# Sorting the tokens on chip with a permuting transposition instead of through rows in DRAM

## The reference, cut to what matters

```python
h = _layernorm(x, axis=-1) * (1 + ca) + sa
x = x + ga * _L0_attn_ref(h, ...)
h = _layernorm(x, axis=-1) * (1 + cb) + sb
x = x + gb * _L0_ffn_ref(h, ...)
...
logits = x_flat @ w_router.T
probs = jax.nn.softmax(logits, axis=-1)
top_idx = jnp.argmax(probs, axis=-1)
top_weight = jnp.take_along_axis(probs, top_idx[:, None], axis=1)[:, 0]
h = jnp.einsum('nd,ehd->enh', x_flat, w_fc)
a = jnp.square(jnp.where(h >= 0, h, 0.5 * h))
expert_out = jnp.einsum('enh,edh->end', a, w_proj)
```

## Time and profile before

| | |
|---|---|
| median of 3 runs | 616.06 us (613.67 to 618.61) |
| profiled execution | span 626.6 us; no other time of it is shown |
| instructions | 11028 |
| PE busy | 545.7 us (87%) |
| DVE busy | 394.7 us (63%) |
| ACT busy | 282.3 us (45%) |
| POOL busy | 209.2 us (33%) |
| moved by DMA | 61.40 MB |

### The profile page before, as it was taken

How to read it: one execution, slowest core, us unless ns; L and a number is a source line. 1 busy time by engine, 2 the same in 40 slices (tenths; PEclk the granted TensorE clock), 3 DMA queues, 4 the chain that set the end, 5 groups by cost and what they waited for, 6 DMA issues and landing times.

```text
span 626.6 us, 11028 instructions
## 1 busy us (share of the span) xinstructions
PE 545.7 (87%) x3052; PEld 441.0 (70%) x3052; DVE 394.7 (63%) x801; ACT 282.3 (45%) x679; POOL 209.2 (33%) x185
## 2 busy tenths in 40 slices
PE   5989959494528899999999999999999999998860
PEld 0435444453327899999999999999999999987750
DVE  3697889898893565454555545555545455567862
ACT  2668583532114455454445445455445445432320
POOL 1030276684886121122122122122112212157541
PEclk9999969789658999999999999999999999999996
DMA  8911543030267520201201202202101010077641
GB/s 314 390 69 52 217 152 120 0 137 1 84 235 236 222 69 2 70 16 51 69 0 67 67 0 67 67 0 67 64 3 67 6 61 0 0 242 245 182 143 67
DMA packets 17042, 61.40 MB, mean 98 GB/s; under 512 B 3051, under 2 KB 3051, under 8 KB 13688
## 3 DMA queue, kind: packets, MB, share of 16 engines
q1 hardware_dynamic: 11256, 42.63, 19.3%
q0 software_dynamic: 5760, 18.43, 8.2%
HBM read 47.30 MB, written 14.27 MB: 98 GB/s over the span
## 4 chain that ended last, share of the span: by engine, by line
PE 71%; DVE 11%; issue 8%; ACT 3%; DMA 2%; another core or an unknown queue 2%; POOL 1%; DVEq 0%; SPq 0%; ACTq 0%; POOLq 0%
PE bank L912 32%; PE bank L940 28%; PE bank L756 3%; DVE xc L1076 3%; PE bank L821 2%; DVE junk L1151 1%; PE bank L774 1%; PE bank L789 1%; PE bank L826 1%; DVE u L1089 1%; DMA sorted_tokens<-gap,gapI 1%; DVE st L1019 1%; DMA wm<-wmod 1%; DVE res L1126 1%
## 5 line engine op out<-in xcount | busy, mean ns | idle before, releaser
L490 POOL TENSOR_TENSOR Wlo<-raw,Whi (+1 forms) x64 | 82.3, 1290 | 276.4 <-ACT Whi L651 276.3
L912 PE MATMUL bank<-XShi,Whi 128*128 (+1 forms) x576 | 165.7, 288 | 5.7 <-DVE twice_h L1341 4.9
L912 PE MATMUL bank<-XShi,Wlo 128*128 (+1 forms) x576 | 164.1, 285 | 0.0
L912 PE MATMUL bank<-XSlo,Whi 128*128 (+1 forms) x576 | 164.1, 285 | 0.0
L1360 DVE TENSOR_TENSOR acc<-acc,bank 128x512 f32 (+1 forms) x126 | 85.9, 687 | 71.7 <-PE bank L940 66.6
L1341 DVE TENSOR_TENSOR twice_h<-relu_h,bank 128x256 f32<-128x256 f32 x144 | 60.2, 420 | 99.4 <-ACT relu_h L713 96.8
L912 PEld LDWEIGHTS bank<-XShi,Whi 128*128 128x128 f32 x576 | 111.6, 194 | 12.1 <-issue 9.8
L940 PE MATMUL bank<-Whi,ahi 128*128 128x512 f32 x272 | 107.9, 397 | 6.6 <-DVE alo L1349 6.5
L912 PEld LDWEIGHTS bank<-XSlo,Whi 128*128 128x128 f32 x576 | 111.6, 194 | 2.1
L912 PEld LDWEIGHTS bank<-XShi,Wlo 128*128 128x128 f32 x576 | 111.5, 194 | 0.0
L940 PE MATMUL bank<-Wlo,ahi 128*128 128x512 f32 x272 | 107.3, 394 | 0.0
(11 more groups left out here) (146 smaller groups left out, 605.9 us busy)
## 6 DMA issues: line engine op xcount, KB each, us to landing
raw<-wffn SPq DMA_DIRECT2D x16, 1024.0 KB, 5.2
wm<-wmod SPq DMA_DIRECT2D x6, 1024.0 KB, 12.4
res_row<-sorted_residuals SPq DMA_DIRECT2D x18, 260.0 KB
sorted_rows<-sorted_tokens SPq DMA_DIRECT2D x9, 512.0 KB, 10.8
x_in<-x SPq DMA_DIRECT2D x4, 1024.0 KB, 10.1
bc<-mod_rows SPq DMA_DIRECT2D x4, 772.0 KB, 7.0
ga_bc<-ga_rows SPq DMA_DIRECT2D x4, 256.0 KB, 3.5
wx_sb<-wx SPq DMA_DIRECT2D x1, 514.0 KB, 10.7
```

The costliest lines, as they stand in the source:

```text
L490: pool.tensor_tensor(Wlo[:, hb % 2, c, :], raw[:, c, :], Whi[:, hb % 2, c, :].bitcast(F32), ALU.subtract).then_inc(s_wlo, 1)
L912: mm = pe.matmul(hP[m][:, 0:TILE], W[wp][:, par, 2 * e + k // 2, o:o + P], XS[xp][:, k, bass.ds(t * TILE, TILE)], start=(n == 0), stop=(n ...
```

## The change

The sorted rows never go to DRAM. A token's place within its block of 128, from the front for one expert and from the back for the other, makes a 0/1 matrix `perm` (four DVE instructions per batch). PE's transposition of z2 takes it in the identity's place, so its result is channels by tokens with the tokens of a block in order: one expert's first, the other's last. ACT evicts this modulated (scale and bias per channel from `cols`) into a window of 128 columns of `XSfull` (channels by sorted tokens, four channel groups innermost) that starts at the front's running count, read from memory into a register; then the whole window is copied to the place that the count from the back gives. The next block overwrites what did not belong. In the last batch DVE makes the copies. POOL clears XSfull first. XShi and XSlo are made from XSfull, with no reload and no transpositions among the expert tiles.

Along with it: the margin comes from `res` times the router row before normalisation, corrected by two numbers per batch, so it no longer needs z2; the modulated router row (`wd_dram`) and the sums (`sc_dram`) are broadcast for all batches at once, and `margin_products(0)` waits for all five landings. POOL has no h2 work. The statistics of the first normalisation are all on DVE (`stats1`), in the places shown. The output of blocks uses two PSUM banks (`pO`) where four were used. Tap 2 of the next batch stands behind the margins and not before them. Ranks and positions of a batch stand together ahead of the next scan. `prefix(b)` stands behind all four transpositions of batch b+2 on PE. The residual rows are still scattered through DRAM.

```diff
...
+            def permuted_block(b, j):
+                n = TJ * b + j
+                if j < 2:
+                    pe.wait_ge(s_hT, KT * min(b + 3, NB))
+                wait(pe, s_e0, KT * (n - 1))
+                pe.wait_ge(s_pm, n + 1)
+                pe.wait_ge(s_z2, n + 1)
+                for k in range(KT):
+                    mm = pe.transpose(pT[j % 2][:, P * k:P * k + P], z2[:, j, P * k:P * k + P], perm[:, j, :])
+                mm.then_inc(s_pz, 1)
...
+            def place(b):
+
+
+                act.wait_ge(s_off, b + 1)
+                first = [act.value_load(offI[0:1, b % 2, j:j + 1], min_val=0, max_val=P * (TJ * b + j)) for j in range(TJ)]
+                if b == 0:
+                    act.wait_ge(s_fill, 1)
+                    act.wait_ge(s_cols, 3)
+                for j in range(TJ):
+                    n = TJ * b + j
+                    act.wait_ge(s_pz, n + 1)
+                    wait(act, s_e1, n)
+                    for k in range(KT):
+                        act.activation(XSfull[:, bass.ds(first[j], P), k], pT[j % 2][:, P * k:P * k + P], ACT.Identity,
+                                       bias=cols[:, 4, k, b:b + 1], scale=cols[:, 3, k, b:b + 1]).then_inc(s_e0, 1)
+                    if b < NB - 1:
+                        act.wait_ge(s_e0, KT * (n + 1))
+                        act.activation(XSfull[:, bass.ds(first[j] + (FROM_BACK - P * n), P), :],
+                                       XSfull[:, bass.ds(first[j], P), :], ACT.Copy).then_inc(s_e1, 1)
...
+            pool.wait_ge(s_wg, NB)
+            pool.wait_ge(s_mr, 7)
+            pool.wait_ge(s_mc, 3)
+            pool.wait_ge(s_md, 64)
+            pool.memset(XSfull[:, :, :], 0.0).then_inc(s_fill, 1)
...
+            def margin_products(b):
+                if b == 0:
+                    dve.wait_ge(s_bc, 16 * (NB + 1))
+                for j in range(TJ):
+                    dve.wait_ge(s_x2, TJ * b + j + 1)
+                    wait(dve, s_q, TJ * b + j)
+                    dve.tensor_tensor_reduce(junk[:, :], res[:, b % 2, j, 0:DM], bc[:, b, :], 1.0, 0.0, ALU.mult, ALU.add,
+                                             q[:, j:j + 1]).then_inc(s_q, 1)
...
+            def permutations(b):
+                wait(dve, s_pz, TJ * b)
+                for j in range(TJ):
+                    dve.tensor_scalar(perm[:, j, :], colidx[:, :], place_col[:, j:j + 1], None, ALU.is_equal).then_inc(s_pm, 1)
...
+            b = NB - 1
+            dve.wait_ge(s_off, NB)
+            first = [dve.value_load(offI[0:1, b % 2, j:j + 1], min_val=0, max_val=P * (TJ * b + j)) for j in range(TJ)]
+            dve.wait_ge(s_e1, TJ * b)
+            for j in range(TJ):
+                n = TJ * b + j
+                dve.wait_ge(s_e0, KT * (n + 1))
+                dve.wait_ge(s_e1, n)
+                dve.tensor_copy(XSfull[:, bass.ds(first[j] + (FROM_BACK - P * n), P), :],
+                                XSfull[:, bass.ds(first[j], P), :]).then_inc(s_e1, 1)
...
```

More of the change, by code:

```diff
@@ new lines, in build @@
+        woutg += [take(f"woutg{b}", [P, DM]) for b in range(2, NB)]
+        wout_sb = take("wout_sb", [P, DM])
+        wdb = take("wdb", [P, KT, P])
+        perm = take("perm", [P, TJ, P])
+        wm = [at(f"wm{n}", [P, KT, 512], F32, o) for n, o in enumerate((o_raw, o_raw + ZB, o_whi, o_whi + ZB, o_wlo, o_wlo + ZB))]
+        cur[0], limit[0] = o_acc, o_a
+        ga_bc = take("ga_bc", [P, NB, DM])
+        modrow = take("modrow", [NB, 6, DM])
+        wdrow = take("wdrow", [NB, DM])
+        scrow = take("scrow", [NB, SC])
@@ L246, in build @@
         s_gbc = sem("ga_broadcast_landed")
[L247 removed]
+        s_bc = sem("router_rows_landed")
         s_md = sem("mod_stored")
@@ L766, in mod_columns, with transposes1 @@
                 mm.then_inc(s_mc, 1)
-            def transposes1(b, ks=range(KT)):
-                for k in ks:
+            def transposes1(b):
+                for k in range(KT):
+                    if k < 2 and b >= 2:
+                        wait(pe, s_e0, KT * TJ * (b - 2))
                     wait(pe, s_hT, KT * b + k - 1)
@@ new lines, in prefix @@
+                pe.matmul(pO[0][:, TJ:2 * TJ], ones[:, :], m1[:, :], start=True, stop=True).then_inc(s_pf, 1)
+            def permuted_block(b, j):
[5 more added lines that the diff above has]
+                pe.wait_ge(s_z2, n + 1)
+                for k in range(KT):
+                    mm = pe.transpose(pT[j % 2][:, P * k:P * k + P], z2[:, j, P * k:P * k + P], perm[:, j, :])
+                mm.then_inc(s_pz, 1)
@@ L1280, in _ @@
                 if nxt:
-                    for k in range(KT):
-                        if k == 2:
-                            softplus_residue(b + 1)
-                        conv(b + 1, 2, (k,), taps)
-                        if newton_steps and k < 3:
-                            newton_steps[k + 1]()
+                    softplus_residue(b + 1)
+                if b == 0:
+                    own.link(mod_row(3, modrow[0:NB, 3, :], 1.0))
+                    dve.tensor_tensor_reduce(wdrow[:, :], modrow[0:NB, 3, :], wdiff[:, :], 1.0, 0.0, ALU.mult, ALU.add,
+                                             scrow[:, 1:2]).then_inc(s_mr, 1)
@@ L1307, in _ @@
-                margins(b)
-                if b == NB - 1:
-                    row_candidates(b)
-                    counts(b)
-                    ranks(b)
-                    positions(b)
+                    columns(3, 5, 3).then_inc(s_cols, 1)
+                if b == 1:
+                    newton1(3)
+                margin_products(b)
+                margins(b)
+                candidates(b)
+                if b == 0:
+                    mod_row(5, modrow[0:NB, 5, :], 0.0).then_inc(s_mr, 1)
+                    dve.wait_ge(s_mr, 6)
+                    clamp_row(5)
@@ L1314, in _ @@
+                if nxt:
+                    conv(b + 1, 2, range(KT), taps)
+                ranks(b)
+                permutations(b)
+                if b == NB - 1:
                     own.link(dve.tensor_scalar(n0f[:, :], run[:, :], -1.0, float(TOK), ALU.mult, ALU.add))
```

611 lines of the change are left out of this document (236 added, 375 removed).

## The result

The changed kernel takes 637.26 us (median of 4 runs, 635.92 to 637.76), the kernel before 617.19 on the same chip (4 runs, 613.67 to 618.61). The ratio is 1.034, 95% interval 1.030 to 1.038: 20.1 us slower. The forecast said 626.0, slower by 10.0, range 609 to 641. The direction and the range held; half of the loss was missing.

What follows compares the result with a forecast made beforehand. DVE was taken to bound the mixer, TensorE the experts. Start -0.4, three batch steps +13.4, +4.2 and -4.1, and tail -3.1 sum to +10.0 us on 616.06, so 626, range 609 to 641.

Steps and rivals of the forecast that it cites:

- Batch 0 to 1: Mixer step from batch 0's decayed state ready to batch 1's: 57.1 us where it was 43.7, +13.4.
- (a): Batch 0 to 1: with two output banks instead of four, DVE waits 4.2 us for delta product, Abs and Exp.
- (c): Batch 0 to 1: all five broadcasts of the packed rows must land, at 80.1 us against 72.77 before.
- (e): Batch 0 to 1: TensorE's prefix counts stand behind all transposes of batch 2, so ranks begin at 94.4 us.
- (g): Batch 0 to 1: state product behind the prefix, partly at TensorE's slow clock; together 5.6 us instead of 3.6.
- The tail: From the last state ready to the experts' effective start: 35.8 us where it was 38.9, -3.1.
- effective start: When expert block 0 would have begun if gapless up to the next block's first fc: 201.8 us before, forecast 211.8.
- rival C: Placing of sorted tokens on ACT is the bound, at 0.73 us an eviction: +25, 641 us; chance 0.13.
- The carried difference: Profiled span of before, 626.6 us, is 10.5 above the runs' median; carried over, giving 616.06 + 10 = 626.
- A: Mixer: DVE stays the bound and the new waits hide, under 4 us a batch: -10, 606 us; chance 0.15.
- B: No change: same chain with fast clock, overlapping register loads and quick broadcasts: +2, 618 us; chance 0.22.
- D: GpSimd's clearing of XSfull holds DVE's small copy of the ranks: +12 in all, 628 us; chance 0.10.

Runs made afterwards that it cites:

- Experiments 5: Changed kernel with tap 2 before the margin products, TensorE's prefix counts before the transposes, XSfull cleared after the first four permutations; 639.88 us, ratio to before 1.012 to 1.033.
- 9: Changed kernel with the edits of Experiments 5, 7, Experiment 2 and experiment 6 together; 617.00 us, ratio to the kernel before 0.980 to 0.996.
- Experiment 2: Changed kernel with GpSimd's four subtractions for weight chunks 4 to 7 delayed until the last block is copied; 642.14 us, ratio to before 1.013 to 1.028.
- Experiment 1: Changed kernel with the high and low passes reading XSfull contiguously, which permutes the tokens; 642.27 us, ratio to before 1.017 to 1.034.
- experiment 6: Changed kernel with block 0's high and low passes of tile t+2 behind tile t's squares and low part; 643.29 us, ratio to before 1.009 to 1.034.
- 10: Kernel 9 with GpSimd's four subtractions of chunks 4 to 7 also behind DVE's first four low passes; 610.29 us, ratio to before 0.991 to 0.997.
- 4: Changed kernel with the delta product before permuted blocks and outputs on TensorE, Abs and Exp before placing on ACT; 650.70 us, ratio to before 1.026 to 1.046.
- 7: As 4, with all four outputs of a batch also ahead of the third and fourth permuted block on TensorE; 641.61 us, ratio to before 1.016 to 1.043.

## Why the prediction was half right

*What bounds the kernel, the start, the three steps.* Right in place and size. Start -0.5 (forecast -0.4). Batch 0 to 1: 56.1 where it was 43.7, +12.4 (+13.4). Batch 1 to 2: +3.7 (+4.2). Batch 2 to 3: -4.2 (-4.1). The named waits of terms (a), (c) and (e) stand in the first step where they were put, in DVE's timeline of after:

```profile
63.58 0.43 DVE L968 TENSOR_SCALAR w<-eabs 128x512 f32<-128x512 f32 x1 [4.03 <-ACT eabs L529]
...
76.90 0.19 DVE L1081 COPY cols<-bank 128x32 f32<-128x32 f32 x1 [2.95 <-PE bank L689]
...
80.32 0.69 DVE L1020 CUSTOM_DVE_ANT_0 eabs<-res,bc 128x512 f32<-128x512 f32 x1 [3.23 <-DMA scal<-router_sums]
...
94.09 0.16 DVE L1043 TENSOR_TENSOR place_col<-cand,bank 128x4 f32<-128x4 f32 x1 [3.52 <-PE bank L748]
```

Product start 80.3 (80.1), ranks 94.1 (94.4). Experiments 5 and 9 confirm (c) and (e) by taking them away. Term (g) was too high in batch 0: the state product took 4.47, not 5.6, and the second Bu did not wait. The close agreement of the last step is partly luck: DVE had Exp's result 1.4 sooner after state ready than forecast and was 0.7 quicker from there to the end of the first Bu, but the state product of batch 3 took 6.47 us and held the second Bu for 1.94, which the sum did not have.

*The eviction* was 1.63 for four, 0.41 each; I had taken 0.40 against bounds of 0.32 and 0.73. The register loads on DVE began 0.73 apart (four from 193.0 to 195.2) where I had 0.8.

```profile
100.73 1.63 ACT L579 ACTIVATE XSfull<-bank,cols 128x128 f32<-128x128 f32 x4 [3.69 <-PE bank L758]
```

*The tail is the step that failed*, "from state ready 35.8 where it was 38.9: -3.1". By the mark (before: effective start 201.8 and mark 281.05, so the mark less 79.25) after's effective start is 222.0, and from state ready 47.8: +8.9, not -3.1. Against the forecast of 211.8 that is 10.2 late. The states were 1.7 early, so the tail itself is 12.0 longer than the sum made it, in these terms:

- "holds DVE's copies: +1.8" was 4.9 (5.33 less 0.43). I charged the price of somewhat over one subtraction; the copy waited for all four. +3.1. Experiment 2.
- "two high and two low passes, half hidden, 2.1": from the last copy's end to the first fc are 3.5, since a pass takes 1.03 instead of 0.60 and 0.69. +1.4. Experiment 1.
- The effective start took block 0 to be gapless behind its first tile, which was assumed and not worked out. From the second tile on they stand 5.6 to 7.3 apart, and TensorE waits 4.5 us for `alo`. Experiments 1 and 6, by two roads, give 4.7 and 5.1 back. This is the largest single miss. The work of one tile on an engine would not have shown it, for it fits into 5.6 us (experiment 6). What had to be followed is the chain from an fc to its projection, and which GpSimd subtraction its last link, `alo`, meets.
- What is left, some 2.5, is for more than half the first tile: 6.63 from the first fc to the second, where an fc takes 2.87, so 3.8 rather than the 2.4 allowed. The rest, about 1, I did not follow up.

Four terms, 12. I had looked for the unknown of the new layout in the strided *write* of the eviction, made it rival C and found it harmless. The strided *read* twice per block was never priced; the notes on a layout must ask who reads it.

*The carried difference.* "I carry the difference over" was sound in the medians (617.2 + 20.2 at the mark gives 637.4) and would have misled in the spans, where an end of 345.6 was set against one of 332.9.

*Rivals.* A (the waits hide) and B fell: waits (a) and (e) and that for the state product come to 7.6, 9.0 and 5.4 us in the three steps, over the 4 from which A decides. Of the three things that B wanted at once none came: the loads stood 0.73 apart, the state products took 4.47 to 6.47 us where before they took 3.60, and the broadcasts landed as forecast. C gave 641, near the result, by a mechanism that is not there: the eviction is 0.41 and in batch 1 placing was done 0.56 us before the delta product. D was half true: the small copy L1045 took 0.15 in the midst of the clearing, but the four permutations 2.72 instead of 0.87. Of these 1.85 us, near D's 2, some 0.4 counted: the state product ended at 98.4, and the second Bu, behind the permutations, began at 98.8. The rule of the Trainium skill that D drew on (SBUF — State Buffer, section Who interferes with whom) fits the permutations and the window copy; on the 128x1 copy the trace does not show it.

*Signs named ahead.* DVE's waits before L968 (4.0, 3.5, 3.5) and before L1043 (3.5, 3.5, none) came as written. The first fc came 31.1 after the last residual, where the sum has 26.1 and 3 more were allowed: the sign set for "wrong" showed the part of the miss that lies ahead of the first fc. The part in block 0 had no sign of its own.

## What to carry to other kernels

Price a new layout at each reader, not only at the writer: here contiguous reads gave 5.9 us back, and the writes cost none that a row shows. When the work of a pipelined loop changes, follow the chain of one iteration of the first block again, with what other engines do beside its links, before calling it gapless; each engine's sum alone does not show it. When several waits follow each other in one in-order queue, removing one tests little (4 moved the mark by +2, 7 by -2.6); remove them together (9 gained 20 us ahead of the last residual), and judge by a mark in the middle of the program when its end varies by more than the effect.

## What the runs showed of the hardware

- A DVE copy between SBUF windows (0.43 us alone) stayed held over four GpSimd subtractions in a row, 5.33 us. It did not slip in between them.
- DVE's subtraction of two SBUF operands, one of them strided, and GpSimd's slowed each other: 1.73 instead of 1.03 and 1.79 instead of 1.24 each (kernels 9 and 10; 2 shows it too). The Trainium skill names this pair as contending (SBUF — State Buffer, section Who interferes with whom), and the trace agrees; I had not looked for it when I moved the subtractions. DVE's 128x128 TENSOR_SCALAR was held by a GpSimd memset, which reads nothing.
- DVE's two `alo` subtractions (128x256, both operands in SBUF) took 1.81 us instead of 0.75 just behind the start of a GpSimd subtraction, which itself took its usual 1.28.
- A strided read of 4 in 16 bytes costs the same 1.03 us on ACT and on DVE for 512 elements; a strided write of 128, none that shows (0.41 with a dynamic offset, between the 0.32 and 0.73 of the earlier trace rows); no run wrote the same elements in sequence.
- From the mark to the end were 333 us or 341 to 348, with all of the difference in the last block and the finish, and the long form came with stalls that have no releaser on the core. It was long in eleven of the twelve traces of the experiments and 334 in one. The difference is more than half the effect of the change: in the first two spans it hid all but 7.6 of the 20 us.
